# The first batch chunk of a fused embedding and cross-network kernel in two halves, and its late weights loaded later

## What is computed

```python
e = jnp.stack([tbl_0[ids[:, 0]], ..., tbl_38[ids[:, 38]]], axis=1)   # (512, 39, 16)
x0, xk, outs = e, e, []
for W in (f0, f1, f2):            # (39*39, 128), (128*39, 128), (128*39, 128)
    z = einsum('bfd,bgd->bfgd', x0, xk).reshape(b, f * g, d)
    xk = einsum('bpd,pm->bmd', z, W)
    outs.append(xk)
z = jnp.sum(jnp.concatenate(outs, axis=1), axis=-1)                   # (512, 384)
h = jnp.concatenate([z, dense_ctx], axis=1)
h = relu(h @ W_top1 + b_top1); h = relu(h @ W_top2 + b_top2); y = h @ W_top3
```

## Time and profile before

| | us |
|---|---|
| median of 3 timed runs | 659.31 (659.17 to 660.02) |
| the profiled execution, its own time | 664.53 |
| its span, from first to last instruction | 662.7 |
| TensorE busy | 620.6 (94% of the span) |
| VectorE, GpSimd, ScalarE busy | 512.5, 502.3, 338.4 |
| first matmul, first strip | 31.07, 44.84 |

### The profile page before, as it was taken

How to read it: one execution, slowest core, us unless ns; L and a number is a source line. 1 busy time by engine, 2 the same in 40 slices (tenths; PEclk the granted TensorE clock), 3 DMA queues, 4 the chain that set the end, 5 groups by cost and what they waited for, 6 DMA issues and landing times.

```text
span 662.7 us, 10828 instructions
## 1 busy us (share of the span) xinstructions
PE 620.6 (94%) x3088; PEld 467.6 (71%) x3088; DVE 512.5 (77%) x1642; ACT 338.4 (51%) x1146; POOL 502.3 (76%) x486
## 2 busy tenths in 40 slices
PE   0179999999999999999999999999999999999998
PEld 0037777777788777777788777777787777778763
DVE  4149898889886788989885788989885789989800
ACT  3015555656463555656463555656462555657602
POOL 5747989899895698889895688989895686666710
PEclk9989999999999999999999999999999999999999
DMA  6466405031311305040412304040412204000000
GB/s 217 107 162 237 131 3 131 4 88 47 88 48 39 94 3 131 3 109 26 101 34 48 85 3 132 3 120 15 104 31 59 74 4 130 0 1 2 0 1 0
DMA packets 57745, 43.38 MB, mean 65 GB/s; under 512 B 37355, under 2 KB 40683, under 8 KB 57558
## 3 DMA queue, kind: packets, MB, share of 16 engines
q1 hardware_dynamic: 51586, 37.99, 19.8%
q0 software_dynamic: 5120, 1.32, 2.6%
q10 hardware_dynamic: 980, 3.39, 1.5%
HBM read 40.74 MB, written 1.94 MB: 64 GB/s over the span
## 4 chain that ended last, share of the span: by engine, by line
PE 91%; issue 3%; another core or an unknown queue 2%; DMA 1%; ACT 1%; ACTq 1%; POOL 0%; DVE 0%; POOLq 0%; DVEq 0%
PE strip L689 22%; PE strip L690 22%; PE strip L693 21%; PE acc L650 14%; PE acc L721 4%; PE strip L707 3%; DMA g_sum<-in_L_rec_f 1%; PE strip L721 1%; PE strip L788 1%; PE acc L658 1%; ACT first L585 1%; PE strip L768 0%; PE strip L783 0%; PE strip L780 0%
## 5 line engine op out<-in xcount | busy, mean ns | idle before, releaser
L481 DVE SCALAR_TENSOR_TENSOR scaled<-strip,x_t,scaled 128x128 f32<-128x128 f32 x1216 | 332.0, 342 | 26.6 <-PE strip L693 24.1
L689 PE MATMUL strip<-w_hi,x_hi 128*128 128x512 f32 (+1 forms) x640 | 296.2, 463 | 4.1 <-ACT x_hi L530 4.1
L690 PE MATMUL strip<-w_lo,x_hi 128*128 128x512 f32 (+1 forms) x640 | 248.9, 389 | 0.0
L693 PE MATMUL strip<-w_hi,x_lo 128*128 128x512 f32 (+1 forms) x640 | 248.0, 388 | 0.0
L378 POOL TENSOR_TENSOR added<-added,product 128x512 f32<-128x512 f32 x128 | 169.7, 1326 | 80.8 <-ACT product L585 74.9
L585 ACT ACTIVATE product<-strip,x_t 128x128 f32<-128x128 f32 x512 | 146.9, 373 | 139.9 <-PE strip L693 132.7
L368 POOL DMA_INDIRECT found<-in_tables,rows x160 | 157.4, 984 | 28.2 <-issue 10.8
L689 PEld LDWEIGHTS strip<-w_hi,x_hi 128*128 128x128 f32 x640 | 121.0, 189 | 52.1 <-issue 20.1
L690 PEld LDWEIGHTS strip<-w_lo,x_hi 128*128 128x128 f32 x640 | 121.3, 190 | 43.2 <-issue 25.3
L693 PEld LDWEIGHTS strip<-w_hi,x_lo 128*128 128x128 f32 x640 | 120.7, 189 | 24.1
L650 PE MATMUL acc<-z,w 117*128 117x512 f32 x224 | 116.3, 604 | 3.2 <-ACT out L560 2.6
(11 more groups left out here) (57 smaller groups left out, 202.7 us busy)
## 6 DMA issues: line engine op xcount, KB each, us to landing
shifted<-x_fields SPq DMA_DIRECT2D x112, 234.0 KB
x_thrice<-x_fields SPq DMA_DIRECT2D x16, 234.0 KB
found<-in_tables,rows POOLq DMA_INDIRECT x160
w<-in_L_rec_f SPq DMA_DIRECT2D x1, 2496.0 KB, 11.4
g_sum<-in_L_rec_f ACTq DMA_DIRECT2D x4, 512.0 KB, 8.0
x_once<-x_fields SPq DMA_DIRECT2D x16, 78.0 KB
x_fields<-found SPq DMA_DIRECT2D x16, 72.0 KB
wt<-in_W_top SPq DMA_DIRECT2D x1, 768.0 KB
```

The source lines that it names most:

```text
L481: dve.scalar_tensor_tensor(into, strip[:, slot_of_strip(q) % Y_BANKS, j, :], x0_t[:, c % 2, s, f:f + 1], onto, ALU.mult, ALU.add).then_inc ...
L689: pe.matmul(into, x1_hi[:, c % 2, columns], hi, start=True, stop=False)
L690: pe.matmul(into, x1_hi[:, c % 2, columns], lo, start=False, stop=False)
L693: pe.matmul(into, x1_lo[:, c % 2, columns], hi, start=False, stop=True).then_inc(strip_ready, 1)
```

## The change

Chunk 0 is cut into two parts of 16 batch rows (256 columns, two subs each), and the chunks are counted as 17 parts, i = 0 and 1 for chunk 0 and i = c + 1 for the others (`part_of`, `chunk_of`).

- The ids of chunk 0 are laid out anew, so that one gather serves eight fields of 16 rows: five gathers bring a half. SyncE waits for five, writes them to a DRAM tensor of their own (`write_half`), and reads them into the left half of the columns (`read(0)`), then the same for the right half, and only then comes chunk 1. The ids have one more row of 10 for the first rows of the tables.
- Ahead of the first strip, products, layer 0 and the split of its result are done for the left half alone. Those of the right half stand among the first sub strips of chunk 0: transposes at slot 2, products at slots 3 to 9, layer 0 at 6 to 12, `high_x1` at 13, `low_x1` at 14, `sum_x1` at 15. The strips of slot 20 and on use it. The work for chunk 1 stands at the late slots (products at 16 to 28, layer 0 at 22 to 34) and its transposes at slot 17.
- ScalarE waits for the ids to be in before it issues its weight loads.
- The late loads stand behind chunk 3's reads in the SyncE queue instead of chunk 1's, and the dense features are transposed in chunk 5 instead of chunk 2.
- 26 gathers stay ahead, and by its new form the rule of gathers for a sub gives the same counts.

```diff
-GATHERS_IN_SUB = [3, 3, 3, 1]
+GATHERS_IN_SUB = 3
...
+HALVES = 2
+HALF_B = CB // HALVES
+HALF_N = N // HALVES
+HALF_AT_ONCE = P // HALF_B
+HALF_GATHERS = GATHERS // HALVES
+HALF_AGAIN = -(-(SHIFTS - 1) // HALF_AT_ONCE)
+FIELDS_IN_HALF = FIELDS + HALF_AT_ONCE * HALF_AGAIN
...
+X0_PARTS = CHUNKS + HALVES - 1
+
+
+def chunk_of(i):
+    return max(i - HALVES + 1, 0)
+
+
+def part_of(c, s):
+
+    return c + HALVES - 1 if c else s * HALVES // SUBS
+
...
+def subs_of(i):
+    per = SUBS // HALVES
+    return range(per * i, per * i + per) if i < HALVES else range(SUBS)
+
...
+def arrivals(i):
+
+    c = chunk_of(i)
+    return c // 2 + 1 + (i > 0 if c % 2 == 0 else 0)
...
+LATE_LOADS_AFTER = 3
+DENSE_IN = 5
...
+TURN_X0_AT = (6, 8)
+X1_AT = (35, 36, 38)
+PRODUCT0_HALF_AT = [3, 4, 5, 6, 7, 8, 9]
+LAYER0_HALF_AT = [6, 7, 8, 9, 10, 11, 12]
+TURN_X0_HALF_AT = (2, 3)
+
+TURN_X0_LATE_AT = (17, 18)
+X1_HALF_AT = (13, 14, 15)
 DIAGONAL_AT = 20
...
+def layer0_at(c):
+
+
+    plans = []
+    if c == 0:
+        plans.append((1, PRODUCT0_HALF_AT, LAYER0_HALF_AT, *TURN_X0_HALF_AT, *X1_HALF_AT))
+    if c + 1 < CHUNKS:
+        late = c == 0 or closes_quarter(c)
+        plans.append((part_of(c + 1, 0), PRODUCT0_LATE_AT if late else PRODUCT0_AT,
+                      LAYER0_LATE_AT if late else LAYER0_AT,
+                      *(TURN_X0_AT if c else TURN_X0_LATE_AT), *X1_AT))
+    return plans
...
+            def write_half(h):
+
+                sp.wait_ge(gathered_half[h], 16 * HALF_GATHERS)
+                of_last = FIELDS - HALF_AT_ONCE * (HALF_GATHERS - 1)
+                for parts, begin, end, row in ((P, 0, HALF_GATHERS - 1, 0),
+                                               (HALF_B * of_last, HALF_GATHERS - 1, HALF_GATHERS, 0),
+                                               (P, 0, HALF_AGAIN, FIELDS)):
+                    row += HALF_AT_ONCE * begin
+                    sp.dma_start(bass.AP(half_fields, (h * FIELDS_IN_HALF + row) * HALF_N,
+                                         [[D, parts], [HALF_AT_ONCE * HALF_N, end - begin], [1, D]]),
+                                 found[0:parts, 0, HALF_GATHERS * h + begin:HALF_GATHERS * h + end, :]
+                                 ).then_inc(written_half[h], 16)
+
...
+            def read(i):
+
+                if i < HALVES:
+                    sp.wait_ge(written_half[i], 16 * WRITES)
+                else:
+                    sp.wait_ge(written, WRITTEN * chunk_of(i))
+                p = chunk_of(i) % 2
+
+                at_least(sp, z0_ready, T0 * (i - 1) if i > 1 else i)
+                sp.dma_start(x0_thrice[:, p, columns_of(i)], shifted_fields(i, 0, PER_TILE, 0)
+                             ).then_inc(thrice_in[p], 16)
+                if i:
+                    once(i)
                 for t in range(T0):
 
-                    at_least(sp, z0_ready, T0 * (c - 1) + t + 1 if c else 0)
-                    sp.dma_start(shifted[0:ROWS, t, :],
-                                 shifted_fields(c, PER_TILE * t, PER_TILE, 1)).then_inc(shifted_in[t], 16)
-                    if c == 0 and t == 1:
-                        once(c)
+                    at_least(sp, z0_ready, T0 * (i - 1) + t + 1 if i else 0)
+                    sp.dma_start(shifted[0:ROWS, t, columns_of(i)],
+                                 shifted_fields(i, PER_TILE * t, PER_TILE, 1)).then_inc(shifted_in[t], 16)
+                    if i == 0 and t == 1:
...
             sp.dma_start(mask[:], a["mask"]).then_inc(mask_in, 16)
-            write(0)
+            write_half(0)
             read(0)
+            write_half(1)
+            read(1)
...
                 write(c)
-                read(c)
+                read(part_of(c, 0))
+                if c == LATE_LOADS_AFTER:
+                    late_loads()
...
-                if k == 0 and c >= E_SLOTS:
-
-                    pool.wait_ge(written, WRITTEN * (c - E_SLOTS + 1))
+                if k == 0 and c == E_SLOTS:
+
+                    for h in range(HALVES):
+                        pool.wait_ge(written_half[h], 16 * WRITES)
+                elif k == 0 and c > E_SLOTS:
...
-                ).then_inc(gathered[c % E_SLOTS], 16)
+                ).then_inc(gathered[c % E_SLOTS] if c else gathered_half[k // HALF_GATHERS], 16)
...
+            act.wait_ge(ids_in, 16)
             act.dma_start(w0[:], a["w0_upper"]).then_inc(w0_in, 16)
             act.dma_start(w0_mirror, a["w0_lower"]).then_inc(w0_in, 16)
...
+                    for i, product_at, _, _, _, _, low_at, sum_at in layer0_at(c):
+                        if n in product_at:
+                            products0(i, product_at.index(n))
+                        if n == low_at:
+                            low_x1(i)
+                        if n == sum_at:
+                            sum_x1(i)
...
+                pe.matmul(acc0[:, columns_of(i)], w0[:, t, :], z0[:, (T0 * i + t) % Z_SLOTS, columns_of(i)],
...
+            def turn_x0(i):
+                c = chunk_of(i)
+                pe.wait_ge(once_in[c % 2], 16 * arrivals(i))
+
+                at_least(pe, out0_ready, i)
+                for s in subs_of(i):
+                    last = pe.transpose(x0_t_bank[i > 0][:, s, :], x0_once[:, c % 2, P * s:P * s + P], ident[:])
                 last.then_inc(x0_t_turned, 1)
...
+                first_strip = s == subs_of(part_of(c, s))[0] and g == 0
                 if first_strip:
-                    pe.wait_ge(x1_hi_ready, c + 1)
+                    pe.wait_ge(x1_hi_ready, part_of(c, s) + 1)
```

More of the change, by code:

```diff
@@ L148, in build_program @@
         w2 = sb("w2", [P, FIELDS, MAPS])
-        ids = sb("ids_sb", [P, CHUNKS + 1, GATHERS], I32)
+        ids = sb("ids_sb", [P, CHUNKS + 2, GATHERS], I32)
         rows = sb("rows", [P, CHUNKS, GATHERS], I32)
@@ L216, in build_program @@
         written = sem("written")
+        gathered_half = [sem(f"gathered_half_{h}") for h in range(HALVES)]
+        written_half = [sem(f"written_half_{h}") for h in range(HALVES)]
         thrice_in = [sem(f"thrice_in_{k}") for k in range(2)]
@@ L603, in _ @@
                     s, g = n // STRIPS, n % STRIPS
-                    if c == 2 and n == KEEP_DENSE_AT:
+                    if c == DENSE_IN and n == KEEP_DENSE_AT:
                         act.wait_ge(dense_turned, 1)
@@ L607, in _ @@
                         act.copy(dense_t[0:D, :], dense_bank).then_inc(dense_kept, 1)
[L608 to L612 removed]
+                    for i, _, _, _, keep_at, high_at, _, _ in layer0_at(c):
+                        if n == high_at:
+                            high_x1(i)
+                        if n == keep_at:
+                            keep_x0_t(i)
                     if c and n == SUMS_AT:
@@ L743, in _ @@
                         last.then_inc(dense_turned, 1)
-                    if c + 1 < CHUNKS:
-                        at = LAYER0_LATE_AT if closes_quarter(c) else LAYER0_AT
-                        if n in at:
-                            layer0(c + 1, at.index(n))
-                        if n == TURN_X0_AT:
-                            turn_x0(c + 1)
+                    for i, _, layer_at, turn_at, _, _, _, _ in layer0_at(c):
+                        if n in layer_at:
+                            layer0(i, layer_at.index(n))
+                        if n == turn_at:
+                            turn_x0(i)
                     if c and n == SUMS_AT:
@@ L828 @@
     arrays["tables"] = np.concatenate(tables)
-    of_chunks = by_gathers(arrays["ids"]).reshape(CHUNKS, CB, AT_ONCE, GATHERS).transpose(2, 1, 0, 3)
-    first_rows = np.repeat(by_gathers(starts[None])[0], CB, axis=0)
-    arrays["ids"] = np.concatenate((of_chunks.reshape(P, CHUNKS, GATHERS), first_rows[:, None]), axis=1)
+    ids = arrays["ids"]
+    of_chunks = by_gathers(ids, AT_ONCE).reshape(CHUNKS, CB, AT_ONCE, GATHERS).transpose(2, 1, 0, 3)
+    of_chunks = of_chunks.reshape(P, CHUNKS, GATHERS).copy()
+    of_halves = by_gathers(ids[0:CB], HALF_AT_ONCE).reshape(HALVES, HALF_B, HALF_AT_ONCE, HALF_GATHERS)
+    of_chunks[:, 0, :] = of_halves.transpose(2, 1, 0, 3).reshape(P, GATHERS)
+    first_rows = np.repeat(by_gathers(starts[None], AT_ONCE)[0], CB, axis=0)
+    first_rows_half = np.tile(np.repeat(by_gathers(starts[None], HALF_AT_ONCE)[0], HALF_B, axis=0), HALVES)
+    arrays["ids"] = np.concatenate((of_chunks, first_rows[:, None], first_rows_half[:, None]), axis=1)
     w0_rows = arrays.pop("L0_rec_f0")
```

171 lines of the change are left out of this document (79 added, 92 removed).

## The result

The change takes 655.3 us (654.86 to 655.72, four runs) where the kernel before takes 659.7 (659.17 to 660.62, four runs): a ratio of 0.993, interval 0.9915 to 0.9945, or 4.4 us less. The forecast was 654.0. The profiled execution of the change took 655.72 us, with a span of 653.8, and needs no correction: it is one of the timed runs.

The account below looks back on a forecast made before the run. TensorE was taken to bound the kernel, with gain only before the first strip: 10.2 us earlier there, less 4.9 coming back in the strips, gives 5.3, so 659.3 - 5.3 = 654.0 us; range 649.8 to 659.5.

Parts of the forecast that it names:

- What bounds the kernel: TensorE holds 91% of the chain and works without a break among strips; gain only from the 44.84 us before the first.
- The profiled and the timed execution: Before and at the first strips: timed runs lack the unexplained 3.23 us and slow strips' 2.4 us; strips start at 41.6.
- Rival 1: Ahead of the first strip: gap and slow strips are real, the shorter start avoids the gap; gain 9.0, 650.3; chance 0.17.
- Step 1: Start of the write-out: ids 2.2 us earlier, gathers land in 3.8, write at 14.9 instead of 21.20; gain 6.3 us.
- rival 2: Start of the kernel: the ids are in no sooner, the write-out's start gains 4.1, total 656.2 us; chance 0.12.
- Step 2: From the write to the first strip: half-size read-back, layer 0 and copy take 13.0 us against 16.9; gain 3.9.
- Rival 3: Read-back ahead of layer 0: half transfers take as long as full ones, 656.5 us; chance 0.08.
- Step 3: Work coming back inside the strips: right half's layer 0, transposes, waits at slots 2 and 17, clock; 4.9 us lost.
- The clock: First strips: TensorE's clock rises between 30 and 33 us, so one strip is slow; 0.5 us lost.
- rival 4: First strips: TensorE's clock stays at half pace longer; 659.2 us (chance 0.08) or 662.3, slower (chance 0.08).
- What would show it: Signs in the trace: first write at 14.9, first strip at 31.4, chunk 1 to the tower each unchanged.
- Step 4: Late loads, dense features, GpSimd's gathers and chunk 1's write and tiles: all covered, cost nothing.

Follow-up runs that it names:

- e6: The kernel before, unaltered, traced on chip 1, where it has no pause: 660.42 us in its own ten runs.
- e12: The change, unaltered, on chip 12, where kernels show the pause: 667.98 us against 664.74 for the kernel before, ratio 1.0045.
- e4: The change without ScalarE's wait for the ids ahead of its weight loads, on chip 6: 670.43 us, ratio 1.0084.
- e11: The change without ScalarE's wait for the ids, as in e4, but on chip 12: 669.48 us, ratio 1.0072.
- e5: The change, unaltered, run and traced again on chip 1: 655.65 us, ratio 0.9937 to the kernel before.
- e1: The kernel before with an unused buffer of 32 bytes a partition behind the ids, on chip 6: 668.5 us against 664.47, ratio 1.006.
- e7: The change with the ids' buffer moved to the end of memory, all other buffers at their addresses of before, chip 1: 654.45 us, ratio 0.9911 to before.
- e8: The change with late loads behind chunk 1's reads and dense features in chunk 2 again, chip 1: 655.55 us against 655.65 for the change.
- e9: The kernel before with 32 unused bytes a partition behind x_lo, so only x_t and later buffers move, chip 12: 664.61 us against 664.74, ratio 1.0.
- e10: The change with e7's addresses and the right half's work at later slots, on chip 12: 666.25 us, ratio 1.0028 to before.
- e2: The change with an unused buffer of 96 bytes a partition behind the ids, on a chip with the pause: 670.13 us, ratio 1.0087.

## Why the prediction was right, point by point

**What bounds the kernel: right.** TensorE is busy for 12.04 + 30.14 = 42.18 of the first 43.20 us behind 28.60, and the gain came from ahead of the first strip alone.

**The profiled and the timed execution: right for this chip, and half wrong as told.** The pause and the slow strips were taken for something that the timed runs don't have. e6 shows before's first strip at 41.38 (41.6 predicted). But the timed runs of chips 6 and 12 do have them: 664.5 and 664.7 us there, as much as the profiled execution of the rows took (664.53). So that execution most likely ran under their conditions and the three timed ones under those of chip 1; which chip either had isn't on record. Rival 1 asked whether the change avoids the pause where it is real, and gave 9.0 us of gain. It is the other way round: the pause grows from 3.2 to 11.3 us (e12).

**Step 1: right in its sum.** The ids were in at 2.79, sooner than the lower bound of 3.2, and the write went at 14.26 (14.9), so rival 2's premise fell. But e4 and e11, which bring the late ids back, still write at 14.78 and 14.24: the two terms of the step are each off and their sum isn't. The ids gave 3.1 us instead of 2.2, the gathers' landing took 4.4 instead of 3.8, and with late ids and the short landing of 1.45, which the step took as a bound, e11 writes at 14.24. That the sum came out is in part luck: the wait for the ids moves both terms, against each other. The gain is that of waiting for five gathers instead of ten.

**Step 2: right in direction, better in size.** From the write to the read-back 2.7 us instead of 3.5, from the read-back to layer 0 5.8 instead of 6.4, layer 0 to its copy 5.1 instead of 6.0, and the copy 0.6 as forecast. Sum 14.2, where 16.5 was taken (3.5 + 13.0): the first strip is 2.9 us sooner than the 31.4 of the forecast, 12.9 ahead of before in place of 10.2. The halves were worth more than half the bytes suggest: `x_once` takes 2.65 us from its issue to the transposes (19.68 to 22.33), 3.67 before (27.40 to 31.07), 1.0 less. The rule of the Trainium skill ("DMA: Bandwidth & Descriptors", section "Anatomy of one DMA") would have given, as an estimate, 0.27 us for the whole read-back; this trace doesn't agree, and the measurement decides. Rival 3 fell with it.

**Step 3: its terms right within 0.3 us each but for the clock's, and one cost of the strips wasn't in it.** The right half's seven pairs cost 3.0 us. Its matmuls follow one strip in each slot, 1.12 to 1.13 us a slot instead of 0.70. Slot 2's wait is 0.53 us in the profiled execution (worked out: the transposes start 0.758 us after the matmul ahead of them instead of 0.233) and 0.8 in e5; 0.5 was forecast. Slot 17's is 0.43 (0.659 instead of 0.233); 0.7 was forecast. The clock costs nothing instead of 0.5, for it was full before the first strip: the matmuls of layer 0 start 0.43 us apart up to 25.77 and 0.22 from 26.03 on, and the granted clock is 1.00 behind 28.60; rival 4 fell. Of the 2.4 us for before's slow strips, 2.3 are shown: from the first strip to the transposes at slot 6 it takes 6.60 us there (44.84 to 51.44) and 4.31 in e6. VectorE's long products (2.11 and 2.00 us instead of 0.69, beside GpSimd's adds) hold TensorE for 1.0 us in the profiled execution, for nothing in e5, and for 0.9 in before (e6): a matter of the run. The lead of e5 over e6 falls by 4.0 us in this stretch; the terms give 3.9: 3.0 + 0.2 + 0.8 + 0.4, and 0.4 for the pace, less 0.9 that before waits.

**The step that failed** is the last clause of "What would show it": "From chunk 1 to the tower each should take what it took". Each takes 0.3 us longer, 4.0 us in all by e1, because a buffer grew by 40 bytes and moved `x_hi` and `x_lo` by 32. The forecast has no term for it. That 654.0 was nearly met is in good part luck: the start gave 2.7 more than forecast, and the pace took 4.0. With the measured terms the sum is 12.9 at the first strip, less 3.0 + 0.2 + 0.53 + 0.43 = 4.2 of step 3, less 0.1 for VectorE's products (1.0 here, 0.9 in before), less 4.0 for the pace: 4.6 of 659.7, or 655.1, and 655.3 was measured. The test that takes the pace away, e7, gains 1.2 us and not 4.0, and it has waits for VectorE that the change hasn't; so 4.0 is what the new addresses cost the kernel before (e1); that they cost the change as much isn't shown.

**Step 4: right.** e8 moves the late loads back and nothing changes. GpSimd's first add starts at 39.21 (about 40 forecast), and chunk 1's write goes at 34.88 (36.7 forecast).

**What the forecast didn't ask** is whether the ground it stood on is the same on each chip. The sign of the gain isn't: 0.7% faster where there is no pause, 0.45% slower on chip 12, where there is one.

## What to carry to other kernels

Before a start is shortened, look at whether the trace of before has a pause that no row explains, and measure on more than one chip, since such a pause can swallow the gain and more. When a buffer grows, keep the others at their addresses, and compare the distance between two like instructions of an untouched stretch: a move of 32 bytes cost the kernel before 4.0 us, nearly what the whole change won. And ask of a load that is held back what it will then fly beside: the one wait gave 2.6 us in the kernel before, where nothing urgent was behind it, and nothing at the first write of the change.

## What the runs showed of the hardware

- The pace of a strip matmul of 512 columns depends on where its data lie: 229.4 to 229.5 ns with `x_hi` and `x_lo` at their old addresses (before, e7, e9, e10), 232.7 to 233.0 with all buffers from `rows` on 32 or 128 bytes further (the change, e1, e2). It is 1.4% of a strip and 4.0 us of the kernel before (e1). The float32 products of layer 0 keep their pace, though `z` moved too. Which of the two buffers and which rule is open.
- The same kernel takes 5 us more on some chips (659.8 on chip 1, 664.5 on chip 6, 664.7 on chip 12): a pause that ends at 38 to 45 us, in which three engines stand and GpSimd goes on, and the half clock of the first strips behind it. The pause lasts 3.2 us in before and 11.3 in the change, the slow strips cost before 2.3. Its cause is open; each chip stands for one group of runs, so chip, time and recording aren't told apart.
- Small loads beside large ones: the ids are in at 2.76 to 2.83 us where the weight loads are held back, and at 5.42 to 6.12 with the weight loads beside them. Five gathers land 1.4 us after the last one's end with the weights done or started early (e4, e11), and 4.3 to 4.4 with the weights in flight (the change, e12).
